# Attention turns with the values multiplied in two halves, the last chunk's norm applied by ScalarE, and its projection placed among the second step's maximum units

## The reference

```
x = x + 0.5 * L0_ffn(layernorm(x))      # 8 experts, one chosen per row
x = x + L0_attn(layernorm(x))
x = x + 0.5 * L0_ffn(layernorm(x))
x = x + 0.5 * L1_ffn(layernorm(x))      # ternary weights
x = x + L1_attn(layernorm(x))
x = x + 0.5 * L1_ffn(layernorm(x))
```

```
q, k, v = heads(x @ wq), heads(x @ wk), heads(x @ wv)
scores = where(causal, q @ k.T, -inf)
y = softmax(scores / sqrt(8)) @ v
```

## Time and profile before

| | us |
|---|---|
| median of 3 runs | 1154.98 |
| range of the runs | 1153.21 to 1155.14 |
| profiled execution, device time | 1150.62 |
| its span, first to last instruction | 1148.8 |

### The profile page before, as it was taken

One profiled execution on the slowest core, in us unless ns is written; L12 is line 12 of the kernel. 1 busy time (PEld: TensorE's weight loads), 2 busy tenths in 40 slices (PEclk: granted clock), 3 DMA queues, 4 the chain that ended last, 5 costly groups with the idle time before them and its releaser, 6 DMA issues.

```text
span 1148.8 us, 34508 instructions
## 1 busy us (share of the span) xinstructions
PE 1052.5 (92%) x14722; PEld 483.3 (42%) x14722; DVE 976.4 (85%) x2310; ACT 661.4 (58%) x852; POOL 99.9 (9%) x123
## 2 busy tenths in 40 slices
PE   5999968999999999999998857799999999999998
PEld 3545533333333333334547735333333333333446
DVE  7787589999999999988545886899999999998853
ACT  3422214556777778777624223255677778787784
POOL 1540010000000000000043251100000000000000
PEclk9999979999999999999999979799999999999999
DMA  5061142000000000000011123210000000000001
GB/s 168 1 261 70 56 139 66 3 2 3 3 2 2 3 2 3 2 3 3 2 40 41 33 83 108 69 39 3 2 2 3 2 3 2 3 2 3 3 3 38
DMA packets 29494, 36.68 MB, mean 32 GB/s; under 512 B 3695, under 2 KB 26389, under 8 KB 29085
## 3 DMA queue, kind: packets, MB, share of 16 engines
q1 hardware_dynamic: 27228, 29.22, 7.6%
q0 software_dynamic: 2112, 5.25, 1.7%
HBM read 15.29 MB, written 18.87 MB: 30 GB/s over the span
## 4 chain that ended last, share of the span: by engine, by line
PE 52%; DVE 38%; issue 4%; ACT 3%; DMA 1%; SPq 1%; POOL 0%; DVEq 0%; ACTq 0%; POOLq 0%
DVE part_max L2212 28%; PE psum L2036 12%; PE psum L2057 11%; PE psum L532 6%; PE psum L2007 6%; PE psum L1685 2%; PE psum L2022 2%; ACT hidden L2151 2%; PE psum L2063 1%; PE psum L2090 1%; PE psum L556 1%; PE psum L1288 1%; DVE xn L208 1%; PE psum L311 1%; PE psum L1276 1%
## 5 line engine op out<-in xcount | busy, mean ns | idle before, releaser
L2212 DVE TENSOR_REDUCE part_max<-psum 128x1 f32<-128x512 f32 (+3 forms) x1120 | 675.6, 668 | 37.7 <-PE psum L2063 22.1
L2151 ACT ACTIVATE hidden<-psum 128x1024 f32<-128x1024 f32 (+3 forms) x640 | 539.1, 896 | 216.6 <-PE psum L2007 215.7
L2057 PE MATMUL psum<-k_slots,q_slots 128*32 128x512 f16 (+3 forms) x5120 | 390.8, 355 | 25.9 <-DVE part_max L2212 14.7
L2036 PE MATMUL psum<-hidden,v_aug 128*9 128x512 f32 (+3 forms) x2560 | 289.3, 528 | 0.1
L2057 PEld LDWEIGHTS psum<-k_slots,q_slots 128*32 128x32 f16 x5120 | 123.5, 95 | 283.0 <-DVE part_max L2212 199.5
L2007 PE MATMUL psum<-q_slots,k_slots 32*128 32x512 f16 (+3 forms) x1472 | 140.8, 328 | 9.2 <-ACT hidden L2151 7.6
L532 PE MATMUL psum<-parts,w_parts 128*128 128x512 f16 x384 | 90.7, 388 | 2.8 <-DVE parts L958 2.8
L2063 PE MATMUL psum<-ident_bf,later_keys 128*32 128x128 bf16 (+2 forms) x1408 | 91.4, 250 | 0.0
L2007 PEld LDWEIGHTS psum<-q_slots,k_slots 32*128 32x128 f16 x1472 | 42.3, 91 | 98.9 <-ACT hidden L2151 47.5
L2022 PE MATMUL psum<-later_keys,ident_bf 128*32 128x128 bf16 x2048 | 74.7, 222 | 3.1 <-DVE v_aug L356 1.4
L2036 PEld LDWEIGHTS psum<-hidden,v_aug 128*9 128x9 f32 x2560 | 61.6, 90 | 34.4 <-ACT hidden L2151 1.5
(11 more groups left out here) (289 smaller groups left out, 841.3 us busy)
## 6 DMA issues: line engine op xcount, KB each, us to landing
expert_regions<-k_slots SPq DMA_DIRECT2D x2, 4096.0 KB, 17.6
q_slots<-q_rows SPq DMA_DIRECT2D x8, 512.0 KB, 3.8
k_slots<-k_rows POOLq DMA_DIRECT2D x28, 128.0 KB, 4.2
q_slots<-in_L_ffn_W_dram SPq DMA_DIRECT2D x2, 1024.0 KB, 6.4
q_rows<-parts SPq DMA_DIRECT2D x6, 256.0 KB, 2.6
k_rows<-parts SPq DMA_DIRECT2D x6, 256.0 KB, 2.7
q_slots<-expert_regions SPq DMA_DIRECT2D x20, 64.0 KB, 1.8
sorted_rows<-xn SPq DMA_DIRECT2D x5, 256.0 KB, 2.3
```

The source lines that it names most:

```text
L2036: last = pe.matmul(psum[VW * h:VW * h + DH + 1, O_BANK, off:CH], v_aug[:, j, G * g + h, :], probs[:, (2 * n + h // 2) % NP, h % 2, off:CH] ...
L2057: last = pe.matmul(psum[rows32(m), bank, a * w:(a + 1) * w], q_slots[:, g, qb * P + m * SLOT:qb * P + (m + 1) * SLOT], k_slots[:, G * g + ...
L2151: act.activation(probs[:, tile % NP, :, off:CH], psum[:, bank:bank + 2, off:CH], ACT.Exp, scale=scale).then_inc(exp_done, 1)
L2212: dve.tensor_reduce(part_max[:, step_no[s] % 2, h0:h0 + heads, i, kc], psum[:, bank, 0:heads * w].rearrange("p (a k) -> p a k", a=heads), ...
```

## The change

There are three parts. First, VectorE no longer applies the late norm: it computes one more small tensor, minus mean times reciprocal deviation, and ScalarE applies scale and bias with four activations. Second, the last chunk's projection moves from after turn 2 into it: transposes before its fourth unit, queries and keys before the sixth, values before the eighth, and VectorE's part of it after the ninth of the eleven units. Third, `values` of a quad is cut at query column 256 into two groups of four matmuls, with one ring item ahead of the first, one between them and the rest behind, wherever the turn has at least three items and the quad before has at least 384 columns.

```
+            def scales(self, dve, scratch, chunk, scaled):
+                lo, hi = chunk * BPC, (chunk + 1) * BPC
+                norm_rstd(dve, dve_chain.on(dve), scratch, 1e-5, lo, BPC)
+                dve.scalar_tensor_tensor(out=scratch.scaled[:, lo:hi], in0=scratch.mean_var[:, lo:hi, 0], scalar=-1.0,
+                                         in1=scratch.rstd[:, lo:hi], op0=ALU.mult, op1=ALU.mult).then_inc(scaled, 1)
+
+            def apply_on(self, act, scratch, chunk):
+                for b in range(chunk * BPC, (chunk + 1) * BPC):
+                    act.activation(xn[:, b, :], x_res[:, b, :], ACT.Identity, bias=scratch.scaled[:, b:b + 1],
+                                   scale=scratch.rstd[:, b:b + 1]).then_inc(self.ready, 1)
...
-            LATE_NORM, LAST_PROJECTION = 1, 3
+            LATE_NORM, LAST_PROJECTION, PROJECTED_BY = 1, 2, 9
...
+                    cols = {0: slice(off, max(off, CH // 2)), 1: slice(max(off, CH // 2), CH)}[side] if halved else slice(off, CH)
                     for h in range(G):
-                        last = pe.matmul(psum[VW * h:VW * h + DH + 1, O_BANK, off:CH],
+                        last = pe.matmul(psum[VW * h:VW * h + DH + 1, O_BANK, cols],
...
-                    if turn == LAST_PROJECTION:
-                        proj.transposes(pe, NCH - 1)
-                        proj.queries_keys(pe, NCH - 1)
-                        proj.values(pe, NCH - 1)
...
+                    halved = bool(previous) and len(items) >= 3 and first_query(previous) < CH // 2
+                    if turn == LAST_PROJECTION:
+                        parts_of_turn = [items, [], []]
+                    elif halved:
+                        parts_of_turn = [items[:1], items[1:2], items[2:]]
...
+                        if place == 3:
+                            proj.transposes(pe, NCH - 1)
+                        if place == 5:
+                            proj.queries_keys(pe, NCH - 1)
+                        if place == 7:
+                            proj.values(pe, NCH - 1)
+                        ring_item(item)
...
                     if previous:
-                        values(previous)
-                    for item in items[half:]:
+                        values(previous, 0, halved)
+                    for item in parts_of_turn[1]:
+                        ring_item(item)
+                    if halved:
+                        values(previous, 1, halved)
+                    for item in parts_of_turn[2]:
                         ring_item(item)
...
-                for n in range(proj.ahead, NCH):
+                for n in range(proj.ahead, NCH - 1):
                     proj.high_parts(act, n)
+                for i, chunk in enumerate(proj.norms.order[given:]):
+                    act.wait_ge(late_scaled, (NCH - given) * layer + i + 1)
+                    proj.norms.apply_on(act, s1, chunk)
+                proj.high_parts(act, NCH - 1)
...
-                            proj.norms.make(dve, own, s1, chunk)
+                            proj.norms.begin(dve, own, s1, chunk)
+                            proj.norms.scales(dve, s1, chunk, late_scaled)
...
+                        if (turn, place) == (LAST_PROJECTION, PROJECTED_BY):
+                            proj.low_parts(dve, NCH - 1)
+                            proj.values_out(dve, NCH - 1)
```

26 lines of the change are left out of this document (15 added, 11 removed).

## The result

The changed kernel takes 1157.49 us (median of 20 runs, 1153.84 to 1159.10) and the kernel before, beside it on the same chip, 1154.03 (1151.12 to 1164.94). The ratio is 1.0028, with a 95% interval of 1.0017 to 1.0039: some 3.2 us slower. A second comparison, made later with the same kernel as an experiment (`change_again`), gave 1.0018 [1.0005, 1.0032]. So the change costs a little, at the edge of what I had called no gain that shows.

The account below looks back on a forecast made before the run. VectorE was taken as the bound in half of layer 0's attention, TensorE and ScalarE alternating later. Terms 1.1 + 1.3 - 0.8 = +1.6 us on a median of 1154.98 gave 1156.6, range 1151.0 to 1160.0.

Parts of the forecast that it names:

- no gain that shows: Whole kernel: projection move and halved values cancel, within 2.3 us either way; the forecast case, chance 0.47.
- the slower one: Rival, chance 0.25: slow-clock queries and keys starve VectorE in both layers, halving returns nothing; +3.4 to +5 us, 1158 to 1160.
- The norm on ScalarE: Late norm: VectorE's path loses 0.9 us; four ScalarE activations take 1.6 us, result ready 0.7 us later.
- The three waits inside turn 2: VectorE waits before units four, six and eight: 1.0, 2.35, 0.35 us in layer 0; about 1.0, 3.1, 0.35 in layer 1.
- The 0.84 us ahead of turn 4 stays: Before turn 4's first unit: VectorE's 0.84 us wait remains, as maximum transpose and two score tiles still stand ahead.
- Sum of the move and the norm: Around turn 2: new waits against savings on VectorE give +1.1 us in layer 0 and +1.3 in layer 1.
- A clock that the change itself touches: Turn 2's sum hangs on the granted clock, 0.50 until 173.9 us in layer 0 and 733.7 in layer 1.
- My sum for full clock: Turn 2, queries and keys at full clock in both layers: waits 0.6, 1.35, 0.35 us, sum -0.3 in layer 0.
- Values in halves: Attention turns: less waiting on the ring and VectorE idling, -0.4 us a layer, -0.8 in all, ends 0 and -3 a layer.
- My own test for being wrong: Wrong if the VectorE-bound stage or the next shortens over 1.5 us a layer, or the projection holds up no unit.
- The cost of the halves: 217 turns with added matmuls: at most 0.01 us a turn, 2.2 us in all; the skill's estimate was 4.3 us.
- The faster one: Rival, chance 0.28: halving returns 1.5 to 3 us a layer, or full clock gains 0.3 a layer; 1149 to 1152 us.

Follow-up runs that it names:

- change_fill2: The changed kernel plus 32 matmuls a layer whose result nobody reads, to keep TensorE busy; 1149.78 us, ratio 0.9963 to the kernel before.
- halves_only: The kernel before with only the values cut in halves, norm and projection unchanged; 1146.70 us against 1149.31, ratio 0.9978.
- norm_halves: The changed kernel with the projection back after turn 2, keeping norm on ScalarE and halved values; 1144.50 us, ratio 0.9939 to the kernel before.

## Why the prediction came out as it did

The time, 1157.49, lies 0.9 us above the forecast of 1156.6 and inside the range. The ratio of 1.0028 lies past the 0.2% that I had set as the bound of no change, so of my three cases it is the slower one, just; the second comparison lies just inside. The closeness is partly luck. Two terms were too small and have opposite signs. And I had added the change to a median before of 1154.98, of three runs, where that of the 20 runs beside the changed kernel is 1154.03: what I forecast was +1.6 us, and what was measured is +3.2 by the ratio (+3.5 by the medians), twice that. It is also just short of the 1158 to 1160 that I gave the slower case.

- **The norm on ScalarE: right.** Predicted 0.9 us off VectorE's path. VectorE's stretch from A to its first maxima shrank from 169.81 - 164.88 = 4.93 us to 168.07 - 164.10 = 3.97, 0.96 us. The four activations took 1.65 us where I took 1.6. The estimate from the Trainium skill ("ScalarE: Activation LUTs", section "What ACT_TABLE_LOAD costs"), 1.64 us, agrees with this row.
- **The three waits inside turn 2: right in kind, and short.** Predicted 1.0, 2.35 and 0.35 in layer 0; measured 1.03, 2.86 and 0.67. Counted from A, queries and keys started at 7.18 us (171.28 - 164.10), not at 6.87 (171.75 - 164.88), and took 3.19 us, not 2.95 (2.15 slow + 0.8), so they ended later against the units. In layer 1 the prediction had 3.1 and the row 3.37, above the 1.3 to 3.1 that I had named as the sign. The values' wait was 0.67 in both layers, and in change_fill2 too, so the low clock isn't its cause.
- **"The 0.84 us ahead of turn 4 stays": this step failed.** VectorE now makes `neg_max` after the low parts and the values' copy, and TensorE, which has finished everything else, waits for it 3.44 us. The transpose of `neg_max`, for which VectorE didn't wait before, is now on VectorE's path (0.55), and the clock has fallen toward the end of the idle time (0.50 from 180.6), so the wait for the first unit is 1.14. Together 1.69 us rather than 0.84. In change_fill2 they are 0.45 + 0.49 = 0.94: the order costs 0.1 us by itself, and the rest of the 0.85 comes with the low clock. The order of the instructions, quoted ahead of the prediction, showed `neg_max` at the end; I didn't ask who waits for it.
- **Sum of the move and the norm.** Predicted +1.1 and +1.3, measured +2.92 and +2.81 from A to B. For layer 0 the waits are 6.25 against the 4.54 that I had counted (1.0 + 2.35 + 0.35 + 0.84), 1.7 us more, and 1.1 + 1.7 = 2.8. The distance that I had named, from the end of the late norm's statistics to the first unit of turn 4, is 183.33 - 167.37 = 16.0 us, not 14.1.
- **A clock that the change itself touches: named, but taken as given.** I had said the sum hangs on it and then used the stretches of before. The change adds a second slow stretch in each layer. My sum for full clock was -0.3 us in layer 0; change_fill2, its fillers included, shows +0.29.
- **Values in halves: a gain as forecast, its size and the argument for it wrong.** Predicted -0.4 us a layer; halves_only shows -1.52 and -1.86 from B to C, and in the full change, where the slow stretch reaches into that stage, -1.37 and -1.26. All of these lie between the ends that I gave the term, 0 and -3, but far from the value that I took from them. Of halves_only's gain in layer 0, the idle time shows 1.1 us; the rest are delays that the overlap of durations hides. And I had argued with turns of four units, where the third unit is issued at the same time; in those of five and six the whole block stood behind the third and kept the fourth back. My own test for being wrong, a stage shorter by more than 1.5 us a layer, isn't met by the change, but it is by halves_only and norm_halves, so that argument of mine was wrong.
- **The cost of the halves: not seen.** From C to D, halves_only takes 134.38 and 132.85 us against 134.32 and 132.83, with 284 and 276 more matmuls. These are net figures: a small gain in the same stage could hide a cost. The Trainium skill's fixed cost on every matmul ("TensorE: Matmul & The Clock Gate", section "Wait — 56ns, not 53.3ns?"), by which I estimated 4.3 us in all, would be an estimated 0.7 us a layer in this stage, and doesn't show here.
- **The rivals.** The slower one named the right price, queries and keys at the low clock, but wanted halving to return nothing. The faster one's halving came true (1.5 to 1.9 us a layer), and without the move it would have been the result: norm_halves is 0.61% faster.

## What to carry to other kernels

Filling a consumer's wait with work from elsewhere pays only if the work fits into the stock between producer and consumer: here a ring of three units can't cover queries and keys with the unit behind them, two were in it at most, and the two waits removed came back as four others. When a small result that another engine turns round (here `neg_max`) is moved behind large jobs, ask what that engine does meanwhile, and what its idle time does to the clock behind it. And cut a long block into the producer's own waits rather than shift it: the cut gained 1.5 to 1.9 us a layer, the shift of the whole block lost 5.3.
